# Row maxima of two heads per VectorE instruction, with four PSUM banks for the maxima and two for the exponentials' scores

## The reference, cut to what matters

```
def _L0_attn_ref(x, wq, bq, wk, bk, wv, bv, wo, bo):
    q = jnp.einsum('bsd,hde->bhse', x, wq) + bq
    k = jnp.einsum('bsd,hde->bhse', x, wk) + bk
    v = jnp.einsum('bsd,hde->bhse', x, wv) + bv
    scores = jax.nn.softmax(jnp.einsum('bhse,bhte->bhst', q, k) * scale, axis=-1)
    att = jnp.einsum('bhst,bhte->bhse', scores, v)
    ...
    return att @ wo.T + bo
...
x = x + _L0_attn_ref(_layernorm(x), ...)      # 16 heads, 512 x 512 scores each
x = x + _L0_ffn_ref(_layernorm(x), ...)       # gate, up, down: 384 hidden
x = x + _L1_attn_ref(_layernorm(x), ...)      # the same with rms-normed q and k
x = x + _L1_ffn_ref(_layernorm(x), ...)       # 8 routed rank-8 adapters
```

## Time and profile before

| | |
|---|---|
| time, median of 3 runs | 2039.91 us (2033.29 to 2040.09) |
| the profiled execution's own time | 2033.34 us |
| its span | 2031.6 us |
| PE busy | 1783.5 us, 88% |
| DVE busy | 1585.8 us, 78% |
| ACT busy | 1425.4 us, 70% |
| POOL busy | 439.0 us, 22% |
| mean granted TensorE clock | 0.966 |

### The profile page before, as it was taken

One profiled execution on the slowest core, in us unless ns is written; L12 is line 12 of the kernel. 1 busy time (PEld: TensorE's weight loads), 2 busy tenths in 40 slices (PEclk: granted clock), 3 DMA queues, 4 the chain that ended last, 5 costly groups with the idle time before them and its releaser, 6 DMA issues.

```text
span 2031.6 us, 32134 instructions
## 1 busy us (share of the span) xinstructions
PE 1783.5 (88%) x10958; PEld 647.2 (32%) x10958; DVE 1585.8 (78%) x3587; ACT 1425.4 (70%) x2921; POOL 439.0 (22%) x579
## 2 busy tenths in 40 slices
PE   4988889989999898988999898998999989898984
PEld 1232333333232333323333232333323333333222
DVE  3878887887888788787878878787787877696871
ACT  2777777776877778676777767677687676675762
POOL 3122112121311213121121311222121121212201
PEclk9999999999999999999999999998999999998996
DMA  6132405041140504114050320504115041121210
GB/s 120 55 79 72 109 18 147 18 116 44 60 111 18 143 18 121 44 50 121 13 140 20 108 63 18 147 18 116 44 49 122 13 128 27 54 50 59 75 34 22
DMA packets 162644, 141.34 MB, mean 70 GB/s; under 512 B 38761, under 2 KB 144050, under 8 KB 162482
## 3 DMA queue, kind: packets, MB, share of 16 engines
q1 hardware_dynamic: 162482, 139.29, 26.4%
HBM read 77.38 MB, written 55.57 MB: 65 GB/s over the span
## 4 chain that ended last, share of the span: by engine, by line
PE 45%; DVE 23%; ACT 13%; DMA 8%; issue 6%; POOL 3%; SPq 2%; DVEq 0%; ACTq 0%; POOLq 0%
DVE neg_max L887 15%; PE ps L1169 14%; PE ps L1154 7%; PE ps L1190 6%; ACT probs L684 6%; PE ps L1143 4%; PE ps L1119 4%; DMA k_stack<-k_rows 4%; PE ps L1234 2%; PE ps L1195 2%; DMA k_rows<-kp 2%; PE ps L1183 2%; PE ps L1240 2%; DVE bn L863 2%; ACT xn L690 1%
## 5 line engine op out<-in xcount | busy, mean ns | idle before, releaser
L887 DVE TENSOR_REDUCE neg_max<-ps 128x1 f32<-128x512 f32 x2048 | 1317.2, 680 | 172.8 <-PE ps L1143 166.9
L684 ACT ACTIVATE probs<-ps 128x512 f32<-128x512 f32 x2048 | 1093.3, 597 | 340.3 <-PE ps L1154 336.7
L1143 PE MATMUL ps<-k_stack,q_stack 48*128 48x512 bf16 x2048 | 696.3, 396 | 78.8 <-DVE neg_max L887 37.6
L1154 PE MATMUL ps<-q_stack,k_stack 50*128 50x512 bf16 x2048 | 659.9, 391 | 56.2 <-ACT probs L684 51.2
L1169 PE MATMUL ps<-probs,v_aug 128*32 128x512 f32 x4096 | 563.1, 622 | 1.9
L1154 PEld LDWEIGHTS ps<-q_stack,k_stack 50*128 50x128 bf16 x2048 | 149.0, 95 | 489.3 <-ACT probs L684 302.4
L1143 PEld LDWEIGHTS ps<-k_stack,q_stack 48*128 48x128 bf16 x2048 | 157.4, 94 | 280.6 <-DVE neg_max L887 227.6
L583 POOL TENSOR_TENSOR o_raw<-o_raw,rden_all 128x512 f32<-128x512 f32 x64 | 81.6, 1276 | 680.2 <-DMA rden_all<-rden_rows 680.2
L564 POOL TENSOR_TENSOR rstd<-vpe,half_neg 128x4 f32<-128x4 f32 x64 | 64.4, 1007 | 355.6 <-DVE vpe L878 355.6
L1169 PEld LDWEIGHTS ps<-probs,v_aug 128*32 128x32 f32 x4096 | 81.8, 109 | 143.9 <-issue 106.0
L690 ACT ACTIVATE xn<-x,shift,rstd 128x128 f32<-128x128 f32 x192 | 80.6, 485 | 28.5 <-POOL shift L566 28.5
(11 more groups left out here) (103 smaller groups left out, 1530.6 us busy)
## 6 DMA issues: line engine op xcount, KB each, us to landing
q_stack<-q_rows SPq DMA_DIRECT2D x128, 192.0 KB, 3.7
k_stack<-k_rows SPq DMA_DIRECT2D x128, 192.0 KB, 4.7
rden_all<-rden_rows SPq DMA_DIRECT2D x64, 256.0 KB
q_rows<-qp SPq DMA_DIRECT2D x32, 384.0 KB, 2.6
k_rows<-kp SPq DMA_DIRECT2D x32, 384.0 KB, 2.8
q_rows<-qp SPq DMA_DIRECT2D x32, 256.0 KB, 2.9
k_rows<-kp SPq DMA_DIRECT2D x32, 256.0 KB, 3.0
x_in<-in_L_attn_x SPq DMA_DIRECT2D x16, 256.0 KB, 4.0
```

The source lines that it names most:

```text
L684: act.activation(probs[:, g % RING, :], ps[:, g % BANKS, :], ACT.Exp).then_inc(exps, 1)
L887: dve.tensor_reduce(neg_max[l][:, pair // 2, col:col + 1], ps[:, BANKS + g % BANKS, :], AX.X, ALU.max, negate=True).then_inc(max_taken, 1)
L1143: pe.matmul(ps[:, BANKS + g % BANKS, :], q_stack[l][row:row + KROWS, pair, tok:tok + 128], k_stack[l][row:row + KROWS, pair, :], start=Tru ...
L1154: pe.matmul(ps[:, g % BANKS, :], k_stack[l][row:row + AROWS, pair, tok:tok + 128], q_stack[l][row:row + AROWS, pair, :], start=True, stop= ...
```

## The change

The six banks are shared out anew: two for the exponentials' scores, four for the maxima. `max_tile` becomes `max_pair`: one reduce reads two neighbouring banks (128 x 2 x 512) and writes two columns of `neg_max`, 16 columns apart. It is emitted in the odd units, and `max_taken` counts pairs. PE waits before an even maximum tile for the pair that lies two pairs back, and before an odd tile for nothing. The exponentials' scores wait for the exponential of score g-2.

```diff
-BANKS = 3
+A_BANKS, M_BANKS = 2, 4
...
-                act.activation(probs[:, g % RING, :], ps[:, g % BANKS, :], ACT.Exp).then_inc(exps, 1)
+                act.activation(probs[:, g % RING, :], ps[:, g % A_BANKS, :], ACT.Exp).then_inc(exps, 1)
...
-            def max_tile(l, b, n):
+            def max_pair(l, b, n):
 
                 g = unit(l, b, n)
-                dve.wait_ge(max_scores, g + 1)
-                pair, st, e = n // 8, (n // 2) % 4, 1 - n % 2
-                col = 16 * e + 4 * (pair % 2) + st
-                dve.tensor_reduce(neg_max[l][:, pair // 2, col:col + 1], ps[:, BANKS + g % BANKS, :], AX.X,
-                                  ALU.max, negate=True).then_inc(max_taken, 1)
+                dve.wait_ge(max_scores, g + 2)
+                pair, st, bank = n // 8, (n // 2) % 4, A_BANKS + g % M_BANKS
+                col = 4 * (pair % 2) + st
+                dst = neg_max[l][:, pair // 2, :].rearrange("p (e c) -> p e c", e=2)
+                dve.tensor_reduce(dst[:, :, col], ps[:, bank:bank + 2, :], AX.X, ALU.max,
+                                  negate=True).then_inc(max_taken, 1)
...
-                dve.wait_ge(max_taken, unit(l, b, 16 * (quarter + 1)))
+                dve.wait_ge(max_taken, unit(l, b, 16 * (quarter + 1)) // 2)
...
                 if a is not None:
-                    max_tile(*a)
+                    if a[2] % 2 == 1:
+                        max_pair(a[0], a[1], a[2] - 1)
...
-                need(pe, max_taken, g + 1 - BANKS)
+                if m % 2 == 0:
+                    need(pe, max_taken, (g - M_BANKS) // 2 + 1)
                 tok, pair, row = 128 * (n % 4), n // 4, HALF * e
-                pe.matmul(ps[:, BANKS + g % BANKS, :], q_stack[l][row:row + KROWS, pair, tok:tok + 128],
+                pe.matmul(ps[:, A_BANKS + (g % M_BANKS) // 2 * 2 + e, :], q_stack[l][row:row + KROWS, pair, tok:tok + 128],
                           k_stack[l][row:row + KROWS, pair, :], start=True, stop=True).then_inc(max_scores, 1)
...
-                need(pe, exps, g + 1 - BANKS)
+                need(pe, exps, g + 1 - A_BANKS)
                 tok, pair, row = 128 * kt, 2 * group + pp, HALF * e
-                pe.matmul(ps[:, g % BANKS, :], k_stack[l][row:row + AROWS, pair, tok:tok + 128],
+                pe.matmul(ps[:, g % A_BANKS, :], k_stack[l][row:row + AROWS, pair, tok:tok + 128],
                           q_stack[l][row:row + AROWS, pair, :], start=True, stop=True).then_inc(scores, 1)
```

## The result

The changed kernel takes 2091.4 us in the median (four runs, 2090.8 to 2107.16). The kernel before, run beside it, took 2036.6 us (four runs, 2028.49 to 2040.09). The ratio over all runs is 1.0295 with a 95% interval of 1.0249 to 1.0341 (the two medians alone give 1.027): the changed kernel is 3% slower. The forecast was 2100 us.

What follows compares the result with a forecast made beforehand. In-order PE, waiting for ACT and DVE at two bank rings, was taken as the bound. 2033.3 + 90 - 35 + 10 = 2098 us, plus 2 for the median: 2100 us; forecast's own range 2060 to 2130, wider range 2020 to 2150.

Steps and rivals of the forecast that it cites:

- What bounds: No engine is full; in-order PE stands before whichever of two rings of three banks, scores or maxima, is full.
- Part 3: Two banks for the exponentials' scores: third and fourth score wait for first and second exponential; 90 us lost, bounds 59 and 103.
- the floor of 1.88 us a group: Least time from first score to value matmuls in groups without a large middle piece, against 1.54 us observed.
- A group with a gate: Group with a gate matmul in its middle: nothing added, 96 such groups in all.
- Parts 1, 2 and 4: DVE side: pair reduce (50 us of DVE time), four maxima banks waited for in pairs (-35 us), order on DVE (+10 us).
- Part 4: Order on DVE: inverse-root steps stand two by two between pairs and expose their waits; 10 us lost, bounds 0 and 20.
- PE's wait before L1157: Sign: PE's wait for ACT before the exponentials' scores (L1154 before the change) grows from 353.6 us to over 450.
- DVE is the bound: Rival: relieving DVE's reduces makes the kernel faster, 1945 us, or 1973 in a milder form; chance 0.19.
- they cancel: Rival: DVE's relief of 57 us and another 30 offset the 90 lost, 2033 to 2045 us; chance 0.11.
- the change doesn't do what it says: Rival: the two-bank reduce runs at half rate or splits, lasting above 1.4 us; 2173 us; no chance of its own.
- Two banks cost more: Rival: second scores also wait (21 us), full 103 lost, no DVE relief, 16 for DVE order; 2173 us; chance 0.20.
- the relief: What the DVE side gives back: -35 us from four maxima banks waited for in pairs, +10 from order on DVE.

Runs made afterwards that it cites:

- first experiment: The kernel before with two banks instead of three for the exponentials' scores, maxima still three banks and single reduces; 2117.86 us, ratio 1.0405.
- second and third experiment: Second: kernel before with two score banks, four maxima banks, single reduces, 2107.78 us (1.0347). Third: changed kernel, each pair reduced by two instructions, 2115.46 us (1.0403).

## Why the prediction was right, step by step

- **What bounds.** It put the waits of in-order PE above the chain's shares. The chain had 15% for the reduce and 6% for the exponential, and the change that served the first at the second's cost lost. The first experiment shows that the shorter ring of the second is the loss.
- **Part 3, the term of +90.** Two score banks alone cost 82 us (1.0405; by the interval 74 to 91), and the floor of 1.88 us a group was met to the hundredth in the changed kernel and in that experiment: none of the 511 groups of the changed kernel is shorter than 1.87 us, where the shortest before took 1.39. A group with a gate as in the earlier trace rows is unchanged, as forecast: 45 of them take 2.46 us in the mean, 2.48 before. Groups with another piece in the middle (transposes of the maxima left aside) did grow, 59 of them by 5 us together, though the prediction added nothing for the large ones. In one gate group of the changed kernel PE goes from the first score of one (995.75) over the gate (996.62) to the value matmuls (998.19), 2.44 us, and 0.31 us lie between fourth score and value matmuls, as in the earlier trace rows:

```profile
995.75 0.39 PE L1157 MATMUL ps<-q_stack,k_stack 50*128 50x512 bf16 x1
...
996.62 1.10 PE L1193 MATMUL ps<-xnt,w_gate 128*128 128x256 f32 x4 [0.17 <-ACT xnt L665]
...
997.88 0.38 PE L1157 MATMUL ps<-q_stack,k_stack 50*128 50x512 bf16 x1
998.19 1.07 PE L1172 MATMUL ps<-probs,v_aug 128*32 128x512 f32 x8
```

- **Parts 1, 2 and 4, -35 and +10.** From the first experiment (1.0405) to the changed kernel (1.0295) the other edits give back 1.1%, 22 us, against 25 forecast; the two intervals leave 5 to 40. How this divides between the fourth bank, the pair instruction and the order on DVE isn't shown: the second and third experiment differ from both neighbours by less than their intervals and the clock allow to tell. The duration of a pair was forecast at 1.23 us and is 1.218. Four queued ones take 4.61 us, so they start (4.61 - 1.22) / 3 = 1.13 us apart, 0.07 less than two single ones (forecast 0.05). The Trainium skill's formula ("VectorE: DVE Perf Modes", "The TRN2 errata"), which is for an fp32 add, would give 0.157 as an estimate, if it held for these reduces from PSUM and nothing overlapped; the measurement decides for 0.07 where reduces are queued.
- **Part 4** shows in the timeline of DVE in the changed kernel, where two chained steps stand side by side and start 0.31 us apart, against the 0.20 after which a reduce followed in the earlier trace rows. The trace has 62 such neighbours, 0.31 us apart in the median, where the prediction counted 112 at 0.34. That makes an estimate of 62 x 0.11 = 7 us, against 10 forecast; no run measured it alone:

```profile
1159.35 0.28 DVE L973 SCALAR_TENSOR_TENSOR nw_u<-nw_t,ms 128x128 f32<-128x128 f32 x1
1159.66 0.29 DVE L976 SCALAR_TENSOR_TENSOR nw_y<-nw_u,nw_y 128x128 f32<-128x128 f32 x1
```

- **What it understated.** PE's wait before L1157 was to pass 450 us, and it is 811. That number adds the idle time of weight load and matmul, and in a plain group the third score, which went without waiting in the earlier trace rows, now waits too. It served as a sign, not as a term of the sum.
- **The rivals.** "DVE is the bound" and "they cancel" fell with the measured 3%, and "the change doesn't do what it says" with the pair's 1.218 us. "Two banks cost more" came out at 2091 us instead of 2173: what the second scores wait beyond 0.23 us behind the first grew from 6 to 12 us over all groups, not by 21.
- **How much is luck.** The loss was forecast at 90 us and measured at 82, the relief at 25 and measured at 22 (5 to 40). Both errors are small, and they cancel in part. The size of the loss is shown; that the relief came out so near is partly luck, given the width of what was measured, and given that the prediction took the middle between 12 and 57 us for its largest part without a reason beyond that.

## What to carry to other kernels

When two rings hold back one in-order engine, price a bank by the time from a burst's first matmul to the last one it lets through: write down, for each ring, when tile n may go (consumer of tile n - depth, done) and take the later. A bank moved from one ring to the other is a trade, and the chain's largest line doesn't tell its sign; lay out one plain group for each choice. And if an in-order engine must wait within a burst, look first whether long independent work can stand there: moving the value matmuls into the wait gained more than any division of the banks tried here. Moving the pieces there gained nothing, so such a place has to be tried.

## What the runs showed of the hardware

- A reduce over two PSUM banks in one instruction runs at the rate of single ones: 1024 columns in 1.218 us, 512 in 0.680, so 1.05 ns a column between the two. The column price of the two evictions in the earlier trace rows, 1.07 ns, forecast 1.23 us, so no cost shows at the border between the banks.
- About half of what a reduce costs beyond its columns is hidden when reduces queue. From start to start it is 0.60 us for 512 columns and 1.13 for 1024, so 0.07 us each beside 0.53 us of columns; by the durations (0.680 and 1.218 us) it is 0.14 us each.
- The mean granted clock of PE scatters between runs of one kernel: 0.954 to 0.970 in the runs of the kernel before, 0.950 to 0.966 with two score banks, 0.961 to 0.966 in the changed kernel. It lay below all runs of the kernel before with two banks for the maxima (0.944 to 0.948), and with the pieces shifted in the kernel before (0.943 to 0.953, and 0.935 to 0.952 with the middle stage too), although the work was the same. How much of each time it explains wasn't separated.
